# Queries of attention 0 copied inside the attention, and scores two tiles ahead in both small attentions

## The reference: what is computed

```python
# attention 0: 16 heads of 32, each query sees keys up to 64 places back
q = apply_rope(q) * d ** (-0.5);  k = apply_rope(k)
scores = jnp.einsum('bhqd,bhqwd->bhqw', q, k_win)
scores = jnp.where(mask, -jnp.inf, scores)
probs = softmax(scores);  ctx = jnp.einsum('bhqw,bhqwd->bhqd', probs, v_win)
x = x + ctx @ o_w.T + o_b
# attention 1: 16 heads of 64, no mask
scores = jnp.einsum('bqhd,bkhd->bhqk', q, k) * SCALE
x = x + jnp.einsum('bhqk,bkhd->bqhd', softmax(scores), v) @ Wo + bo
```

## Time and profile before

| | us |
|---|---|
| median of 3 runs | 1541.66 (1541.19 to 1542.73) |
| the profiled execution, its own time | 1541.65 |
| its span, first to last instruction | 1539.5 |
| TensorE busy | 1428.5 (93% of the span) |
| VectorE busy | 709.0 (46%) |
| ScalarE busy | 507.1 (33%) |
| GpSimd busy | 365.1 (24%) |
| mean granted TensorE clock | 0.953 of full speed |

### The profile page before, as it was taken

One profiled execution on the slowest core, in us unless ns is written; L12 is line 12 of the kernel. 1 busy time (PEld: TensorE's weight loads), 2 busy tenths in 40 slices (PEclk: granted clock), 3 DMA queues, 4 the chain that ended last, 5 costly groups with the idle time before them and its releaser, 6 DMA issues. The chain is left out here.

```text
span 1539.5 us, 26558 instructions
## 1 busy us (share of the span) xinstructions
PE 1428.5 (93%) x11152; PEld 1051.7 (68%) x11152; DVE 709.0 (46%) x1309; ACT 507.1 (33%) x835; POOL 365.1 (24%) x228
## 2 busy tenths in 40 slices
PE   7787989798989899999999999999999998997995
PEld 3565876444446688888888887888888875434773
DVE  2366868977735332223322323233223333675832
ACT  0324412322212143253333432524324344523702
POOL 6102010000021332222312231313132211315911
PEclk9778978999999999999999999999999999899997
DMA  5211210100214211121111110111112016003000
GB/s 201 102 63 76 90 42 1 76 1 0 82 62 134 66 56 55 33 62 33 51 37 57 39 55 27 62 33 56 55 34 62 23 46 243 15 0 130 0 1 27
DMA packets 49572, 88.01 MB, mean 57 GB/s; under 512 B 28584, under 2 KB 41136, under 8 KB 46128
## 3 DMA queue, kind: packets, MB, share of 16 engines
q1 hardware_dynamic: 49456, 86.32, 16.1%
HBM read 76.61 MB, written 9.70 MB: 56 GB/s over the span
## 5 line engine op out<-in xcount | busy, mean ns | idle before, releaser
L1257 POOL TENSOR_TENSOR ctx_hi<-ctx_raw,one 128x1536 fp32r<-128x1536 f32 (+1 forms) x32 | 91.5, 2858 | 566.0 <-DMA ctx_raw<-in_ctx 379.8
L1455 ACT COPY ET<-PS 128x512 f32<-128x512 f32 (+1 forms) x224 | 129.6, 585 | 277.0 <-PE PS L1359 201.8
L1558 DVE TENSOR_SCALAR_CACHE_REDUCE E<-PS 128x384 f32<-128x384 f32 (+1 forms) x256 | 131.8, 572 | 180.5 <-PE PS L1336 179.9
L1527 DVE TENSOR_TENSOR V<-PS,vbias 128x512 f32<-128x512 f32 (+1 forms) x104 | 71.8, 691 | 193.0 <-PE PS L1303 192.8
L1303 PE MATMUL PS<-ctx_raw_r,wk_hi 128*128 128x384 f32 (+1 forms) x512 | 128.1, 355 | 0.0
L1303 PE MATMUL PS<-wv_lo,ctx_hi 128*128 128x512 f32 (+1 forms) x416 | 127.6, 406 | 0.0
L1462 ACT ACTIVATE E<-E,peak 128x1601 f32<-128x1601 f32 x64 | 103.5, 1623 | 66.9 <-DVE peak L1563 66.9
L1359 PE MATMUL PS<-ident,E 128*128 128x128 f32 (+1 forms) x832 | 123.1, 273 | 0.4 <-issue 0.4
L1303 PE MATMUL PS<-ctx_hi,wk_hi 128*128 128x384 f32 (+1 forms) x512 | 120.6, 357 | 1.5 <-POOL ctx_raw_r L1260 1.5
L1303 PE MATMUL PS<-wv_hi,ctx_hi 128*128 128x512 f32 (+1 forms) x416 | 120.4, 411 | 0.8 <-POOL ctx_raw_r L1260 0.8
L1260 POOL TENSOR_TENSOR ctx_raw_r<-ctx_raw,ctx_hi 128x1536 fp32r<-128x1536 f32 (+1 forms) x32 | 116.9, 3654 | 2.5
(11 more groups left out here) (296 smaller groups left out, 2201.3 us busy)
## 6 DMA issues: line engine op xcount, KB each, us to landing
ctx_raw<-in_ctx SPq DMA_DIRECT2D x24, 768.0 KB, 4.3
ctx_raw<-in_ctx_first SPq DMA_DIRECT2D x8, 900.0 KB, 4.5
rel_scr<-rel_out SPq DMA_DIRECT2D x8, 640.0 KB, 3.7
fwk<-in_fwk SPq DMA_DIRECT2D x1, 4096.0 KB, 12.2
fwv<-in_fwv SPq DMA_DIRECT2D x1, 4096.0 KB, 13.9
corr<-rel_scr SPq DMA_DIRECT2D x64, 48.0 KB
p_scr<-E SPq DMA_DIRECT2D x16, 192.0 KB, 2.3
near<-p_scr SPq DMA_DIRECT2D x64, 48.0 KB
```

What stands on the lines that cost most here:

```text
L1257: nc.gpsimd.tensor_tensor(ctx_hi[r][:, :, 0:n], ctx_raw[r][:, :, 0:n], one[:].unsqueeze(1).broadcast_to([P, KC, n]), ALU.mult).then_inc(S[ ...
L1455: nc.scalar.copy(ET[0:n, j % ET_RING, :], src[0:n, :]).then_inc(S["et_out"], 1)
L1527: v.tensor_tensor(V[0:rows, at % V_RING, :], bank(4 + NUMBER[unit] % 2)[0:rows, :], vbias[0:rows, :], ALU.add).then_inc(S["v_out"], 1)
L1558: v.tensor_scalar(E[:, p, k0:k0 + n], bank(r)[:, 0:n], 1.0, None, ALU.mult, ALU.max, accum_out=tops[:, p, c:c + 1]).then_inc(S["s_out"], 1)
```

## The change

A small class `Queries` takes over the copies of the queries. ScalarE copies tile 0's queries at the end of `local_projections`, as before, and tiles 1 to 3 as the first thing in attention 0, in front of the first exponential. scores(t) of attention 0 waits for eight copies per tile (semaphore bq0_in). In both small attentions TensorE's stream becomes scores(0), scores(1), and then for each t: values(t), scores(t+2), context(t), project(t-1); at the end project(3). The streams of VectorE, GpSimd and SP are not edited.

```diff
--- before.py
+++ after.py
@@ -137,6 +137,27 @@
     return last
 
 
+class Queries:
+
+
+    def __init__(self, nc, s, turned, ready):
+        self.nc, self.s, self.turned, self.ready = nc, s, turned, ready
+
+    def scalar(self, act, t):
+
+        act.wait_ge(self.turned, t + 1)
+        for h in range(4):
+
+            rows = slice(32 * h, 32 * h + 32)
+            for b in range(2):
+                self.nc.scalar.copy(self.s.BQ[rows, h // 2:HP:2, 2 * t + b, (h % 2) * SQ:(h % 2 + 1) * SQ],
+                                    self.s.bank(4 + t)[rows, :].rearrange("p (g b q) -> p g b q", g=KC, b=2)[:, :, b, :]).then_inc(self.ready, 1)
+
+    def tensor(self, pe, t):
+
+        pe.wait_ge(self.ready, 8 * (t + 1))
+
+
 def local_projections(nc, sem, s):
 
 
@@ -167,6 +188,7 @@
             ch.link(eng.tensor_tensor(tv[:, :, 1, :], yv[:, :, 0, :], over(rope[:, 2, :], 1, NH), ALU.mult))
             return eng.tensor_tensor(out[:, t, :], out[:, t, :], tmp[:, :], ALU.add)
 
+        queries = Queries(nc, s, qt_ps, sem("bq0_in"))
         block = ctx.enter_context(nc.Block())
 
         @block.sync
@@ -222,14 +244,7 @@
                 nc.scalar.copy(s.KT[:, 0:KC, t * P:(t + 1) * P],
                                bank(t).rearrange("p (g n) -> p g n", g=KC)).then_inc(kq_in, 1)
             act.wait_ge(bq_zero, 1)
-            for t in range(NT):
-                act.wait_ge(qt_ps, t + 1)
-                for h in range(4):
-
-                    rows = slice(32 * h, 32 * h + 32)
-                    for b in range(2):
-                        nc.scalar.copy(s.BQ[rows, h // 2:HP:2, 2 * t + b, (h % 2) * SQ:(h % 2 + 1) * SQ],
-                                       bank(4 + t)[rows, :].rearrange("p (g b q) -> p g b q", g=KC, b=2)[:, :, b, :]).then_inc(kq_in, 1)
+            queries.scalar(act, 0)
 
         @block.gpsimd
         def _(pool):
@@ -263,9 +278,10 @@
                 dve.wait_ge(q_out, t + 1)
                 rotate(nc.vector, ch, yq, rq, tq, t).then_inc(q_roped, 1)
                 dve.wait_ge(q_roped, t + 1)
-
-
-def small_attention(nc, sem, s, name, dh, scale, mask, w_out, out_bias, prefetch, at, nm, pt_at=None, beside=None):
+    return queries
+
+
+def small_attention(nc, sem, s, name, dh, scale, mask, w_out, out_bias, prefetch, at, nm, pt_at=None, beside=None, queries=None):
 
 
 
@@ -297,6 +313,8 @@
         @block.tensor
         def _(pe):
             def scores(t):
+                if queries:
+                    queries.tensor(pe, t)
                 if t >= 1:
                     pe.wait_ge(s_free if mask else shifted, t)
                 for b in range(2):
@@ -335,14 +353,14 @@
                 linear_to_tokens(nc, bank(6 + t % 2), oT, t, s.w[w_out], 0, D, groups).then_inc(y_ps, 1)
 
             pe.wait_ge(s.loaded[w_out], 16)
-            scores(0)
-            for t in range(NT):
-                if t + 1 < NT:
-                    scores(t + 1)
+            scores(0), scores(1)
+            for t in range(NT):
+                values(t)
+                if t + 2 < NT:
+                    scores(t + 2)
+                context(t)
                 if t >= 1:
                     project(t - 1)
-                values(t)
-                context(t)
             project(NT - 1)
 
         @block.vector
@@ -408,6 +426,9 @@
                 act.wait_ge(shifted, t + 1)
                 nc.scalar.activation(sc[:, t % 2], sc[:, t % 2], ACT.Exp, scale=scale).then_inc(exped, 1)
 
+            if queries:
+                for t in range(1, NT):
+                    queries.scalar(act, t)
             exponentials(0)
             for t in range(NT):
                 if t + 1 < NT:
@@ -2162,9 +2183,9 @@
         norm = lambda name: Norm(nc, sem, s, name)
         n1, n2, n3, n4, n5, n6, n7 = (norm(f"n{k}") for k in range(1, 8))
         with nc.cleanup_on_exit():
-            local_projections(nc, step, s)
+            queries = local_projections(nc, step, s)
             small_attention(nc, step, s, "a0_", 32, 32 ** -0.5, True, "w0o", "ob", [(n, s.w[n][:], dram[n]) for n in ("w1k", "w1q", "w1v")],
-                            s.tail, n1)
+                            s.tail, n1, queries=queries)
             self_projections(nc, step, s, n1)
             rounding = WeightRounding(nc, step, early, s)
             small_attention(nc, step, s, "a1_", 64, 64 ** -0.5, False, "w1o", "bo",
```

## The result

The changed kernel took 1559.68 us (median of 4 runs, 1557.12 to 1562.7) against 1542.1 for the kernel before: a ratio of 1.0114, 95% interval 1.0101 to 1.0126. It is slower by 17.6 us; 1561 was forecast, in a range of 1549 to 1569. The profiled execution took 1562.7 us with a span of 1560.6, 21.1 us more than the span before.

A forecast was written before the change was run, and what follows sets the result against it. Attention 0 was taken as a ring through three engines, behind a gap for query copies, with barriers passing stage gains or losses to the end. 1541.65 + 4.5 (attention 0 with gap) + 15.0 (attention 1) = 1561 us, range 1549 to 1569.

The forecast's parts named there:

- The start: Ahead of attention 0: 24 of 32 query copies move behind the barrier, 7.8 us off the front; scores(0) start at 58.45.
- the spare time ahead of the exponential: ScalarE in attention 0: moved copies end at 66.3, first exponential not wanted before 68.3, so 2.0 us to spare.
- The gain of the early scores and its loss: Attention 0: scores(2) start 14.6 us earlier, but VectorE waits for project(0) until 99.1; 2.9 us are left.
- The ring: One tile's chain, soften through exponential, context, project, residual to weigh, nothing overlapped: 17.0 us in attention 0, 20.4 in attention 1.
- Attention 0 with its gap: Attention 0 plus the gap ahead of it: ends at 133.4 against 128.91 before, +4.5 us.
- Attention 1: Second small attention: early scores gain 5.4 us, then waits for project; ends at 305.9 against 290.91, +15.0 us.
- my list of signs: Expected profile: among others, VectorE waits for project ahead of residual, some 13 us once in attention 0, about 9 a tile after.
- The rule against the row: Scores(2), scores(3), both attentions: whether transposes raise the clock; 1.2 GHz taken, otherwise each up to 3.3 us shorter.
- (a): Rival: clock 2.4 GHz from the first project on; attention 0 -0.4, attention 1 +9.7, so 1551 us; chance 0.12.
- (b): Rival: clock 1.2 GHz nearly throughout, projects 7 and 10.02 us; +10.5 and +20, so 1572 us; chance 0.08.
- (c): Rival, faster: clock stays 2.4 GHz through scores(0) and everything after; attention 0 -11.1, attention 1 -3.4, 1527 us; chance 0.05.
- (d): Rival, no change: the start's gain of 8 to 9 us and small waits cancel; chance 0.03.

The follow-up runs named there:

- project behind context alone: Kernel before with only project(t-1) moved behind context(t), scores one tile ahead and queries as before: 1570.69 us.
- project first: Changed kernel with project(t-1) put back in front of values(t), scores two tiles ahead and queries part kept: 1527.24 us.
- late residual: Changed kernel with only VectorE's residual moved one tile later, residual(t-2) in iteration t: 1525.24 us.
- stands filled: Changed kernel with idle matmuls, results unused, in TensorE's stands ahead of values(2), values(3) and context(2): 1552.64 us.
- values-project: Changed kernel with VectorE's residual one tile later and TensorE's order values(t), project(t-1), scores(t+2), context(t): 1519.35 us.
- attention 0 only: Changed kernel with TensorE's old order back in attention 1, so new order and queries part in attention 0 only: 1541.50 us.
- changed again: Second measurement of the changed kernel, without an edit: 1557.03 us, runs from 1551.55 to 1565.47.

## Why the prediction was right, point by point

- **The start.** scores(0) begin at 59.03, 58.45 was said. 0.44 us of that is the stage before, which ran later in this execution (ScalarE's first query copy at 55.97 instead of 55.53). The copies took 0.326 us each from start to start, as they had alone (0.327), and the spare time ahead of the exponential was 2.15 us (2.0 was said); doubling them brought the delay out. Only five of the 24 ran beside a read of PSUM by VectorE (the mask addition, 65.05 to 66.27 us); their mean duration was 362 ns, that of the others 361. With that agrees the sentence of the Trainium skill (page "PSUM — Partial Sum Buffer", Specifications) that ScalarE and VectorE read PSUM in parallel at full bandwidth while they are in different banks.
- **The gain of the early scores and its loss.** scores(2) 74.98 to 81.95 (74.7 to 81.6 said), project(0) over at 99.27 (99.1), the probabilities of tile 2 at 103.67 (103.4) and of tile 3 at 120.89 (120.4). The ring took 17.2 us, 17.0 was said. Attention 0 with its gap came to +4.9 us, +4.5 was said. Three runs break it or make it alone, each with the sign that was expected: project behind context alone +28.9 us, project first and late residual -32 and -34 us from the changed kernel.
- **Attention 1.** The start was 1.4 us further on than forecast (213.41 against 207.48 + 4.5). The whole was +15.2 us, +15.0 was said, but terms in it were off both ways and cancelled, which is luck. Counted from the attention's start, project(0) was over at 46.5 us (48.2 said), because scores(0) took 3.75 us and not the 5.02 of before, and scores(1) 6.31 and not 7.09. The ring gave back 0.4 us (20.85, 20.4 said), with a context(2) of 3.32 us instead of 2.6. The way from the probabilities of tile 3 to residual(2) gave back 1.6 (15.6, 14.0 said), with a context(3) of 3.32 and a project(2) of 9.4 instead of 8.8. The profile of the second measurement has 12.1, so the forecast's term holds for one course of the clock rather than for the kernel. Of the waits ahead of L373 the first was as said (12.09, 11.5 said); for the others my list of signs said "about 9 a tile", which is true of attention 0 (9.29, 9.56) and was never worked out for attention 1 (4.57, 6.01), where the rounding covers a part.
- **The rule against the row.** I had taken 1.2 GHz for scores(2) and scores(3) and kept up to 6.6 us in each attention as the other end. The first profile showed the one; the second showed 2.4 GHz in most of scores(2) and in scores(3) of attention 0, and ended that attention 7.9 us earlier. That 1.2 GHz came in all four in the run that was forecast is in part luck. In the second profile the granted clock was still 0.50 from 75 to 76 us, a little behind the eight transposes of values(0), and 0.85 from 76 to 77, inside scores(2); the same eight left it low in the other profiles, so that they raise it isn't shown here. The sentence of the Trainium skill ("TensorE: Matmul & The Clock Gate", Part 4), that transposes don't count as busy for the clock in the same way, does not hold everywhere in these traces. In the kernel before, the stage behind attention 1 starts with TensorE at 1.2 GHz after 4.68 us of standing and gives it only 128x128 transposes, issued by the same call as those of values; the granted clock was 0.50 up to 295 us and 0.97 in the next one:

```profile
292.15 3.40 PE L939 MATMUL PS<-ident,wg 128*128 128x128 f32 x16 [4.68 <-PEq L2164]
295.70 1.17 PE L939 MATMUL PS<-ident,wg 128*128 128x128 f32 x8 [0.16 <-ACT wgT L917]
```

- **The rivals.** (a), a high clock from the first project on, is what filling the stands was to make of the kernel: 1552.6, 1551 was said. The filled kernel's one profile, the fastest of its runs, has other parts than (a), though: attention 0 ends 7.9 us earlier than before and attention 1 is 11.2 longer, where (a) had -0.4 and +9.7. (b), (c) and (d) did not come; (c) would have needed the clock to hold in scores(0), and it fell within them in every profile (5.1 to 6.4 us instead of 3.8).

What was not forecast is 1.0 us in the projections between the attentions (76.01 against 74.97). It is the clock again. TensorE's long stream of matmuls there begins about 6 us into the stage, and in the 4 us from then on and in the next 4 the granted clock was 0.63 and 1.00 before, 0.50 and 0.81 after. Eight other profiles have it too (75.8 to 76.1 us), among them the one without the queries part; stands filled and values-project have 75.06 and 74.99 us, as before, with 0.57 and 1.00, and 0.64 and 1.00.

## What to carry to other kernels

When an instruction is moved back in one engine's stream, look in the other engines' streams for what stands right behind its reader: here a norm's residual, itself in no hurry, held up the softmax of the next tile. Such a move has a partner, moving the reader back as well; with both, and the project in front of the next scores, a change that cost 17.6 us became a kernel that is 23 us faster than the one before. Of these 23, the queries part alone is 6.9.

## What the runs showed that I had not expected

One program with one input has two courses of the clock through attention 0. With the same instructions ahead of them, scores(2) took 6.97 us in three profiles (changed, project first, values-project) or 4.05 to 4.41 in four (late residual, filled, attention 0 only, changed again), and the attention then ended up to 7.9 us apart. When scores(0) start, 58.49 to 59.92 us, does not sort them in one order: 59.92 belongs to those with the short scores and 59.57 to those with the long. Nor does the moment at which the clock falls inside scores(0), worked out from the granted clock of windows of 1 us: 59.2 to 59.3 us and 62.1 in the four with the short scores, 60.2, 60.5 and 61.3 in the three with the long. What decides isn't shown. A single profile of such a kernel shows one of the courses. The runs scatter accordingly: those of changed again and of the two kernels with the new order in one attention lie 14 to 16 us apart, those of all others 1.5 to 8.3 us. Attention 1 has its share in that, since the kernel with the new order there alone scatters by 14 us.
